# One-hot batches on three engines in the fold, and one meeting of the engines fewer ahead of the spread, in a four-layer graph network

## The reference

```python
# edge_index = [src, dst], dst sorted; edge_attr = edge_attr_2; weight: [4, 4, 32, 32]
bu = _tent_basis(edge_attr[:, 0], 4)          # max(0, 1 - |u - c_k| / h), 4 centres
bv = _tent_basis(edge_attr[:, 1], 4)
basis = (bu[:, :, None] * bv[:, None, :]).reshape(-1, 16)
xj = x[edge_index[1]]
w2 = weight.reshape(16, 32, 32)
msg = sum(basis[:, k:k + 1] * (xj @ w2[k]) for k in range(16))
out = jax.ops.segment_sum(msg, edge_index[0], num_segments=n_nodes)
x = _layernorm(x + out, axis=-1)
```

## Time and profile before

| what | value |
|---|---|
| median of three runs | 17495.23 us (17494.18 to 17500.92) |
| profiled execution | 17499.07 us, of which the span is 17497.3 us |
| VectorE busy | 12714.1 us, 73% of the span |
| GpSimd busy | 12574.8 us, 72% |
| TensorE busy (matmul) | 6372.7 us, 36% |
| ScalarE busy | 3721.7 us, 21% |

### The profile page before, as it was taken

How to read it: one execution, slowest core, us unless ns; L and a number is a source line. 1 busy time by engine, 2 the same in 40 slices (tenths; PEclk the granted TensorE clock), 3 DMA queues, 4 the chain that set the end, 5 groups by cost and what they waited for, 6 DMA issues and landing times. The chain is left out here.

```text
span 17497.3 us, 146366 instructions
## 1 busy us (share of the span) xinstructions
PE 6372.7 (36%) x33457; PEld 4980.7 (28%) x33457; DVE 12714.1 (73%) x18056; ACT 3721.7 (21%) x6097; POOL 12574.8 (72%) x13055
## 2 busy tenths in 40 slices
PE   1111111110444444444320000000006888888885
PEld 0000000000333333333320000000005777777774
DVE  7777777774899999999663333333337999999996
ACT  1000000000222222222751111111112222222221
POOL 7777777777677777777127777777777777777775
PEclk9999655555777777777665555555558999999997
DMA  6333333331111111111332222222222222222221
GB/s 162 97 97 95 97 99 97 97 95 45 29 28 28 28 28 27 27 28 24 145 122 59 59 59 59 59 59 59 59 52 47 53 55 54 53 55 54 53 56 35
DMA packets 801746, 1107.09 MB, mean 63 GB/s; under 512 B 422003, under 2 KB 564265, under 8 KB 788794
## 3 DMA queue, kind: packets, MB, share of 16 engines
q0 software_dynamic: 422176, 503.42, 13.1%
q1 hardware_dynamic: 303551, 402.93, 8.3%
q10 hardware_dynamic: 75736, 197.70, 3.0%
HBM read 715.27 MB, written 389.49 MB: 63 GB/s over the span
## 5 line engine op out<-in xcount | busy, mean ns | idle before, releaser
L1872 POOL DMA_INDIRECT s_arena<-d_t,s_arena x6250 | 5902.9, 944 | 2015.3 <-issue 1901.2
L1844 POOL DMA_INDIRECT s_arena<-d_t,s_arena x3125 | 3065.9, 981 | 1019.1 <-issue 933.0
L1821 POOL DMA_INDIRECT d_pay<-s_arena x3125 | 3026.8, 969 | 992.3 <-issue 934.7
L1580 PE MATMUL psall<-s_arena 128*128 128x500 bf16 x1875 | 870.5, 492 | 4252.1 <-DVE s_arena L583 3842.8
L1493 ACT ACTIVATE s_arena<-s_arena 128x800 f32<-128x800 f32 x250 | 429.1, 1716 | 6161.2 <-DVE s_arena L1163 6161.2
L1684 PE MATMUL psall<-s_w2r,s_arena 128*128 128x384 f32 x4750 | 1708.1, 493 | 7.5 <-DVE s_arena L1027 6.6
L960 DVE TENSOR_TENSOR s_arena<-s_arena,psall 128x2400 f32<-128x2400 f32 x125 | 332.0, 2656 | 1739.5 <-DMA s_arena<-d_t,s_arena 1739.5
L1580 PEld LDWEIGHTS psall<-s_arena 128*128 128x128 bf16 x1875 | 198.8, 106 | 4825.1 <-DVE s_arena L583 4263.0
L1684 PEld LDWEIGHTS psall<-s_w2r,s_arena 128*128 128x128 f32 x4750 | 1430.7, 315 | 87.6 <-DVE s_arena L1027 18.7
L1770 PE MATMUL psall<-s_tails,s_mfix 128*128 128x32 f32 x6 | 1.9, 412 | 3972.0 <-DVE s_tails L1171 3972.0
L1036 DVE TENSOR_REDUCE s_arena<-s_arena 128x64 f32<-128x1024 f32 x1000 | 1397.4, 1408 | 0.0
(11 more groups left out here) (289 smaller groups left out, 17064.9 us busy)
## 6 DMA issues: line engine op xcount, KB each, us to landing
s_arena<-d_t,s_arena POOLq DMA_INDIRECT x9375, 2.5
d_scan<-s_arena ACTq DMA_DIRECT2D x375, 400.0 KB, 2.5
s_arena<-d_ew SPq DMA_DIRECT2D x126, 800.0 KB
s_arena<-d_pay SPq DMA_DIRECT2D x33, 1650.0 KB, 6.8
d_inj<-s_agg SPq DMA_DIRECT2D x125, 400.0 KB, 4.0
s_arena<-d_inj SPq DMA_DIRECT2D x125, 400.0 KB, 3.4
d_pay<-s_arena POOLq DMA_INDIRECT x3125
d_pay<-s_agg SPq DMA_DIRECT2D x100, 429.0 KB, 3.0
```

Source lines behind the costliest of these rows:

```text
L1580: e.matmul(R5s[:, 0:4], lhsT, rhs[:, 0:4], start=start, stop=True, skip_group_check=True)
L1821: e.indirect_dma_start(pay_d, bass.IndirectOffsetOnAxis(ap=S1.adr[s4][:, t:t + 1], axis=0), S1.pay[s4][:, 33 * t:33 * t + 33], None).then_ ...
L1844: e.indirect_dma_start(L3.gb[s][:, t], None, T3_d, bass.IndirectOffsetOnAxis(ap=L3.idx[s][:, t:t + 1], axis=0)).then_inc(sem(f"g3_{s}"), 16)
L1872: e.indirect_dma_start(L.gb[s][:, t * L.CW:(t + 1) * L.CW], None, L.tab, bass.IndirectOffsetOnAxis(ap=L.idx[s][:, t:t + 1], axis=0)).then_ ...
```

## The change

Three things are done. In the fold, GpSimd makes the one-hots of batch 1 with 20 compares; ScalarE makes those of batch 3 and, in even chunks, of batch 2; VectorE those of 0 and 4 and, in odd chunks, of 2. The first edges' rows are no longer stored into `inj_d`: ScalarE copies them into the scan's first position in chunk 0. And one of the two meetings ahead of the spread is left out; the gathers into the payload buffers and of the first edges' rows are issued before the third part of the scatters, the weight loads before SyncE's wait for the scatters, and ScalarE's layout of the weights and VectorE's fills stand before the meeting that is left.

```diff
@@ vector_chunk2
-            vector_rows2(e, c, i_, k, 2)
+            if k % 2:
+                vector_rows2(e, c, i_, k, 2)
+            else:
+                e.wait_ge(dv.h, v2_rows(c, 2) - 1)
+                e.sem_inc(dv.up(), 1)
@@ scalar_chunk1
-            e.activation(S1.siv[s2][:, :, 1:T + 1].rearrange("p f t -> p t f"), S1.inj[s4].rearrange("p (t f) -> p t f", t=T), ACT.Copy)
+            if i is None:
+                e.wait_ge(sem("ld_d0"), 16)
+                e.activation(S1.siv[0][:, :, 1:2], frow[:, :].unsqueeze(2), ACT.Copy)
+            t0 = 1 if i is None else 0
+            e.activation(S1.siv[s2][:, :, 1 + t0:T + 1].rearrange("p f t -> p t f"), S1.inj[s4][:, 32 * t0:].rearrange("p (t f) -> p t f", f=32), ACT.Copy)
@@ scalar_spread
-            barrier(e, "scalar")
             e.wait_ge(sem("ld_wt1"), 64)
             e.activation(S1.wt.rearrange("p (o a) -> p o a", a=4), S1.wl.rearrange("p (a o) -> p o a", a=4), ACT.Copy).then_inc(sem("p1_w"), 1)
+            barrier(e, "scalar")
@@ scalar_chunk2
-            for b in (1, 3):
+            for b in (3,) if k % 2 else (2, 3):
@@ tensor_chunk2
-                if b in (0, 2, 4):
+                if b in (0, 4) or b == 2 and k % 2:
                     e.wait_ge(dv.h, v2_rows(c, b))
+                elif b == 1:
+                    e.wait_ge(sem("po_rows"), c + 2)
                 else:
-                    e.wait_ge(sem("q_a"), c * 2 + (b + 1) // 2)
+                    e.wait_ge(sem("q_a"), c * 2 + (b - 1))
@@ gpsimd_spread
-            for s in range(4):
-                e.indirect_dma_start(
-                    S1.pay[s][:, 0:32], None, scan_d, bass.IndirectOffsetOnAxis(ap=fe[:, 0:1], axis=0)).then_inc(sem(f"sc{s}"), 16)
@@ new functions of GpSimd
+        def gpsimd_chunk2(e, c, i, k):
+            s2 = k % 2
+            e.wait_ge(sem(f"ro1_{s2}"), nth2(0 if i is None else i, k) * 16)
+            held(e)
+            e.wait_ge(sem("q_y"), c * 5 + 7)
+            held(e)
+            for g in range(4):
+                for j in range(5):
+                    m = e.tensor_scalar(F1.OHv[1][:, g, j], io125[:, 0:NJ], F1.rowv[s2][:, g, 5 + j, 32:33], None, ALU.is_equal)
+            m.then_inc(sem("po_rows"), 1)
+
+        def gpsimd_fold(e):
+            barrier(e, "gpsimd")
+            gpsimd_chunk2(e, 0, None, 0)
+            with e.Fori(0, NC1 // 4) as i:
+                for k in range(1, 5):
+                    gpsimd_chunk2(e, i * 4 + k, i, k)
@@ gpsimd_ends_of
+                    if b == 2:
+                        e.wait_ge(sem("st_x1"), 64)
+                        e.indirect_dma_start(frow[:, :], None, X1_d, bass.IndirectOffsetOnAxis(ap=d0i[:, :].bitcast(U32), axis=0)).then_inc(sem("ld_d0"), 16)
+                        for s in range(4):
+                            e.indirect_dma_start(
+                                S1.pay[s][:, 0:32], None, scan_d, bass.IndirectOffsetOnAxis(ap=fe[:, 0:1], axis=0)).then_inc(sem(f"sc{s}"), 16)
...
-                e.wait_ge(sem("st_x1"), 64)
-                e.indirect_dma_start(frow[:, :], None, X1_d, bass.IndirectOffsetOnAxis(ap=d0i[:, :].bitcast(U32), axis=0)).then_inc(sem("ld_d0"), 16)
@@ each engine's program: one barrier less between *_ends_of(e, 0) and *_spread(e)
-            barrier(e, "vector")
             vector_spread(e)
@@ sync_spread
             barrier(e, "sync")
-            for b in range(4):
-                e.dma_start(S1.wl[32 * b:32 * b + 32].rearrange("p (a o) -> p a o", o=32), W1[:, b].rearrange("a i o -> i a o")).then_inc(sem("ld_wt1"), 16)
@@ sync_ends_of
+                for q in range(4):
+                    e.dma_start(S1.wl[32 * q:32 * q + 32].rearrange("p (a o) -> p a o", o=32), W1[:, q].rearrange("a i o -> i a o")).then_inc(sem("ld_wt1"), 16)
                 e.wait_ge(sem("injs"), 16 * NJ)
-                e.wait_ge(sem("ld_d0"), 16)
-                e.dma_start(inj_d[0:E, :].rearrange("(p t) f -> p t f", p=P)[:, 0], frow[:, :]).then_inc(sem("st_d0"), 16)
-                e.wait_ge(sem("st_d0"), 16)
```

More of the change, by code:

```diff
@@ L612, in vector_starts @@
             mk["starts"] = dv.n
-            e.wait_ge(sem("po_tid"), 1)
+            e.wait_ge(sem("po_rows"), 1)
             e.tensor_copy(tid[0:NP], tid_i[0:NP]).then_inc(dv.up(), 1)
@@ L1349, in scalar_chunk2 @@
                         m = e.activation(F1.OHv[b][:, g, j], io125[:, 0:NJ], ACT.Abs, scale=-1.0, bias=F1.rowv[s2][:, g, 5 * b + j, 32:33])
-                m.then_inc(sem("q_d"), 1)
-                e.wait_ge(sem("q_d"), c * 2 + (b + 1) // 2)
-                e.activation(F1.OH[b], F1.OH[b], ACT.Relu, scale=-1.0, bias=ones[:, 0:1]).then_inc(sem("q_a"), 1)
+                m.then_inc(sem("q_d"), 1 + k % 2)
+                e.wait_ge(sem("q_d"), c * 2 + (b - 1))
+                e.activation(F1.OH[b], F1.OH[b], ACT.Relu, scale=-1.0, bias=ones[:, 0:1]).then_inc(sem("q_a"), 1 + k % 2)
             if i is not None:
@@ L1779, in tensor_program @@
             tensor_ends_of(e, 0)
-            barrier(e, "tensor")
             tensor_spread(e)
@@ L1878, in gpsimd_ends_of @@
             if layer == 0:
-                e.iota(tid_i, [[1, 27]], base=0, channel_multiplier=27).then_inc(sem("po_tid"), 1)
+                e.iota(tid_i, [[1, 27]], base=0, channel_multiplier=27).then_inc(sem("po_rows"), 1)
             if layer != 1:
@@ L1912, in gpsimd_program @@
             gpsimd_ends_of(e, 0)
-            barrier(e, "gpsimd")
             gpsimd_spread(e)
             barrier(e, "gpsimd")
-            barrier(e, "gpsimd")
+            gpsimd_fold(e)
             gpsimd_ends_of(e, 1)
@@ L1979, in sync_spread @@
                     sync_chunk1(e, i * 4 + k, k)
-            e.wait_ge(sem("ld_wt1"), 64)
         def sync_chunk2(e, c, k):
@@ L2096, in sync_program @@
             sync_ends_of(e, 0)
-            barrier(e, "sync")
             sync_spread(e)
```

## The result

The changed kernel took 17466.69 us (median of 20 runs, 17456.10 to 17472.62) where the kernel before took 17494.55 beside it (20 runs, 17486.40 to 17500.92): a ratio of 0.9984 [0.9977, 0.9990], 27.9 us or 0.16% less. The forecast was 17465.6 us, a gain inside 0.2%. The profiled execution took 17470.63 us, its span 17468.2, which is 29.1 less than before.

The account below looks back on a forecast made before the run. GpSimd bounds the spread; VectorE and ScalarE are equally full in the fold. 25.8 us from the fold plus 3.8 from the meeting make 29.6 us less, 17465.6 us; range 17452 to 17488.

Parts of the forecast that it names:

- The batch that VectorE loses: Fold: 16 even chunks each 1.61 us shorter, 13.31 instead of 14.92, with a 0.45 us wait for TensorE; 25.8 us.
- upper bound: Fold: most that VectorE's lost batches could gain, TensorE always at the high clock and no wait; 33.0 us.
- lower bound: Fold: least that VectorE's lost batches could gain, TensorE always at the low clock, GpSimd apart; 25.8 us.
- ScalarE: Fold: its batches stay hidden, 22.7 us per pair of chunks against VectorE's 28.2, with 3 us to spare.
- GpSimd's compares: Fold: 20 compares of 128x100 at 0.29 us, 5.8 us a chunk, hidden.
- the circle: GpSimd's round in the fold: 20 compares plus about 2.1 us, against 14.1 a chunk; free up to 0.60 us a compare.
- The meeting: Ahead of the spread: one meeting fewer, weight loads earlier, less ScalarE's copy; 3.8 us, bounds 1.7 and 9.5.
- A: Fold and meeting: TensorE's batch 0 at the high clock, or a short drain; both give 42.5 us, 17452.7; chance 0.19.
- first leg: Fold: TensorE's batch 0 meets the high clock in even chunks; alone it makes the total gain 36.8 us, 17458.4.
- B: Fold: GpSimd becomes the bound from 0.60 us a compare, at TensorE's wait ahead of batch 1; 17708 us at 0.97; chance 0.08.
- C: Fold: VectorE and GpSimd get in each other's way in SBUF, costing 49 us, 17515 us; chance 0.08.
- D: Fold: waits for TensorE take back the whole batch's time in even chunks, leaving only 3.8 us, 17491 us; chance 0.03.

Follow-up runs that it names:

- without the drain: Changed kernel, with GpSimd adding to the semaphore without draining at the meeting ahead of the spread and the first behind it; 17467.03 us, 0.9975 of before.
- late wait: Changed kernel, with VectorE's wait for TensorE's matmuls placed last of the three waits ahead of batch 0's sums; 17465.73 us, a single run.
- the run with 30 compares: Changed kernel with ten more GpSimd compares a chunk, into a tile nobody reads; 22536.26 us on a slow chip, single run, fold 585.6 us.
- the kernel with TensorE filled: Changed kernel with five matmuls of 500 columns, which nobody reads, behind batch 4 of every chunk; 17468.78 us, a single run.
- batch 4 early with the joined increment: Changed kernel, even chunks' batch 4 made early, its increment joined to batch 0's last sum, matmul wait last, no GpSimd drain at three meetings; 17560.59 us.
- fold-only kernel: Kernel before with only the fold's new split of one-hot batches, both meetings and the store kept; 17489.27 us against 17511.14, 0.9987.
- The last pair of kernels: Changed kernel with early batch 4, joined increment, late matmul wait and three GpSimd drains removed, without and with three increments behind VectorE's fold; 17560.59 and 17442.86 us.
- with batch 4 early: Changed kernel, with VectorE's one-hot batch 4 of even chunks moved ahead of batch 0's sums; 17478.65 us, 0.9980 of before.

## Why the prediction was right

*The batch that VectorE loses* was forecast at 25.8 us and measured at 25.8, but not by the same sum, and that the two agree is luck. The mechanism held: 17 batches fewer, chunk 0 barely shorter, 16 even chunks, odd ones unchanged, a wait for TensorE at the low clock. The term mis-sized is "At the low clock a sum can start 1.97 us after its matmuls do", and with it "VectorE is ready at 1.73: 0.45 us late". In even chunks it starts 2.20 us after. The 1.97 was read at a sum that waits for TensorE alone; batch 0's passes two more waits behind that one, which is 0.15 of the difference (2.05 with TensorE's wait last), and 0.08 stay open. The wait is 0.69 us, an even chunk 13.55 and not 13.31, and the 16 chunks give 16 x 1.37 = 21.9. The rest was no part of the forecast: 0.7 us in chunk 0 (17.93 against 18.62; it varies, since the kernels without the drain and with the late wait show 18.62 too), and 3.0 us in one chunk of before in which TensorE began late, after idle time that the profile puts down to issue. In the timeline of before, TensorE and VectorE there:

```profile
8526.79 6.64 PE L1656 MATMUL psall<-s_arena 128*32 128x100 f32 x170 [4.46 <-issue]
...
8527.94 1.74 DVE L802 SCALAR_TENSOR_TENSOR s_arena<-s_arena,psall 128x100 f32<-128x100 f32 x5 [2.90 <-PE psall L1656]
```

The kernel with only the meeting changed has it too (that chunk takes 18.17 us there, 17.92 before), those with the new fold don't. 21.9 + 3.0 + 0.7 = 25.6. "The semaphore increment [...] lies inside that wait" holds, since the low clock makes TensorE the later of the two; but it costs 0.30 us where TensorE is out of the way, and VectorE's own way is 0.48 long. So the upper bound, "33.0 (always high, no wait)", was wrong: with TensorE at the high clock an even chunk is still 13.33 us, which gives 16 x 1.59 = 25.4; and the lower bound, 25.8, lay above the measured 21.9.

*ScalarE* was forecast as hidden with room, and is: 71.8 us idle in front of its rows.

*GpSimd's compares* were forecast at 0.29 us; they take 0.51 from start to start. The nearest kind by name, the affine select, was a poor guide. The error cost nothing, because 0.51 still lies under the threshold of the circle: 0.60 forecast, 0.60 worked out from the run with 30 compares. That the price stayed there was partly luck: the margin taken for a factor of two was 0.60/0.51.

*The meeting* was forecast at 3.8 us and measured at 3.5 (3.53 and 3.50 with and without the new fold). The drain ended 8.6 us after the last transfer instruction, where 8.3 was taken; at 4402.8 it released the engines about when it had before, since the first layer ended 2 us later.

*The rivals.* A fell on both legs: the low clock stayed, and the drain kept its length. Its first leg would have been worth 3.5 us (25.4 less 21.9) and not 7.2 (36.8 less 29.6), by the kernel with TensorE filled. What A would have brought could be had in part otherwise: removing the drain gave 7.4 us at that meeting where A's bound had 5.7 (9.5 less 3.8; it took 2.7 us from the last scatter to SyncE, which needs 1.4: 4399.4 to 4400.8 in the kernel without the drain), and batch 4 early with the joined increment brought even chunks to 12.96 us, near the 12.86 of a fold without a wait. B was nearer than its 8 in 100 says, and is real: four compares more and the fold is 12.8 us longer than in the changed kernel, ten and it is 109. C is refuted by the sums' mean of 318 ns in both kernels (319 with 30 compares a chunk), and by the fifteen in a row, 5.27 us in both. The Trainium skill (SBUF — State Buffer, Who interferes with whom), which lets a VectorE instruction with at most one SBUF input run beside GpSimd, agrees, with the pointer scalar not counted. D is refuted by the fold-only kernel's 477.4 us.

*The bound.* The range's lower end, 17452, assumed that nothing outside the touched stages moves. The last pair of kernels shows that it can, by 111 us. What follows the fold differed by 2.6 us between before and after, and by -6.0 to +6.2 between before and the experiments of one or two edits (8548.7 without the drain, 8560.9 with batch 4 early). Ahead of the fold the first layer's end differed by some 10 us and the spread by 7, as told above. So several us of a single profiled execution belong to no term of the sum, and that this forecast came out within 1.1 us of the median is partly luck.

## What to carry to other kernels

Price a new stage as a circle with its threshold, and not by a duration alone: the compare was mis-priced by 1.75 times and the forecast held, because it still lay under the price up to which the circle says it is free. A drain of GpSimd at a meeting is a cost in itself when its transfers are already waited for by their own semaphore; a plain increment gave 7.4 us at one meeting and 5.5 at the next. When a small edit to one stage moves the time of a stage that it doesn't touch, look for "issue" idle time in that stage's loop and move the code by a few instructions before the edit is judged; one pair of kernels here shows how much that can be.

## What the hardware showed that was not expected

- GpSimd's drain lasts 6.18 to 6.19 us with everything landed, and ends 8.3 to 8.6 us after the last instruction of a long run of indirect transfers when it was begun among them; repeated at once it takes 0.04 us.
- A compare of 128x100 on GpSimd takes 0.51 us from start to start, 0.46 with a constant, where the one affine select of 128x128 in the trace takes 0.29.
- Three waits in a row cost VectorE 0.16 us more when the one that is met last stands first. A wait for its own last result and an increment cost it 0.30 us where nothing hides them.
- Three increments on VectorE, outside any loop, moved an unchanged loop by some 110 us.
- One chip ran the kernel before in 22423.93 us, with idle time put down to "remote"; nothing here explains it.
